# The head of a two-layer graph kernel: order of TensorE's uses, of the loads on two queues, and of ACT's steps

## What is computed

```
def _L0_gnn_ref(h, adj, simlar, W_proj, b_proj, W_gcn, b_gcn):
    sim = jnp.tanh(adj * simlar)                    # simlar is adj: tanh(adj^2)
    filt = sim * (adj > 0).astype(sim.dtype)
    ...                                             # the T = 350 largest of each row
    h2 = jnp.tanh(h @ W_proj + b_proj)
    feat = jax.nn.relu(new_adj @ (h2 @ W_gcn) + b_gcn)
    return feat

def _L1_gnn_ref(feats, node_adj, edge_adj, node_weight, node_bias, edge_weight, edge_bias):
    pos = jnp.matmul((node_adj > 0).astype(feats.dtype), feats)
    neg = jnp.matmul((node_adj < 0).astype(feats.dtype), feats)
    node_output = jnp.matmul(jnp.concatenate([pos, neg], axis=1), node_weight)
    node_output = node_output + node_bias * jnp.diagonal(edge_adj)[:, None]
    edge_output = jnp.matmul(jnp.matmul(edge_adj, feats), edge_weight)
    return node_output + edge_output + edge_bias * jnp.diagonal(node_adj)[:, None]

x = _layernorm(x + _L0_gnn_ref(x, adj, adj, ...), axis=-1)
x = _layernorm(x + _L1_gnn_ref(x, adj, adj, ...), axis=-1)
```

## Time and profile before

| | us |
|---|---|
| median of 3 runs | 619.83 |
| lowest and highest of them | 618.65, 620.12 |
| the profiled execution's own time | 618.95 |
| its span, first to last instruction | 617.2 |
| busy in the span: PE, DVE, ACT, POOL | 603.0, 472.7, 417.5, 186.9 |

### The profile page before, as it was taken

One profiled execution on the slowest core, in us unless ns is written; L12 is line 12 of the kernel. 1 busy time (PEld: TensorE's weight loads), 2 busy tenths in 40 slices (PEclk: granted clock), 3 DMA queues, 4 the chain that ended last, 5 costly groups with the idle time before them and its releaser, 6 DMA issues.

```text
span 617.2 us, 5685 instructions
## 1 busy us (share of the span) xinstructions
PE 603.0 (98%) x1970; PEld 344.5 (56%) x1970; DVE 472.7 (77%) x683; ACT 417.5 (68%) x297; POOL 186.9 (30%) x80
## 2 busy tenths in 40 slices
PE   7799999999999999999999999999999999999995
PEld 6644444444444444555555655655655656558994
DVE  2577879797887879986787697796787786887733
ACT  3387686868686786648884783883893884865850
POOL 0387796978879796200000000000000000000000
PEclk9799999999999999999999999999999999999998
DMA  8999999999999990047898399387486685783000
GB/s 236 336 343 343 336 281 314 273 327 276 323 292 309 291 236 1 1 137 193 234 248 241 107 252 254 100 244 220 135 252 174 172 243 147 210 242 110 2 17 19
DMA packets 141181, 130.65 MB, mean 212 GB/s; under 512 B 9443, under 2 KB 141158, under 8 KB 141158
## 3 DMA queue, kind: packets, MB, share of 16 engines
q1 hardware_dynamic: 74982, 66.22, 38.9%
q10 hardware_dynamic: 66176, 64.17, 37.4%
HBM read 128.27 MB, written 2.10 MB: 211 GB/s over the span
## 4 chain that ended last, share of the span: by engine, by line
PE 95%; DMA 2%; ACTq 1%; ACT 1%; DVE 0%; issue 0%; DVEq 0%
PE acc L939 36%; PE acc L953 33%; PE stage L962 10%; PE stage L961 10%; PE stage L953 2%; DMA x_rows<-in_x_dram 2%; PE to_rows L968 1%; PE to_rows L967 1%; ACTq L462 1%; PE stage L907 1%; PE to_rows L924 1%; ACT a_cols L525 0%; PE to_cols L913 0%; PE stage L902 0%; ACTq L465 0%
## 5 line engine op out<-in xcount | busy, mean ns | idle before, releaser
L592 DVE STREAM_TRANSPOSE a_cols<-a_rows 128x2048 f32<-128x2048 f32 x128 | 294.5, 2306 | 87.8 <-PE stage L962 53.0
L939 PE MATMUL acc<-a_cols,rhs 128*128 128x512 f32 x512 | 221.1, 592 | 0.7 <-ACT a_cols L525 0.7
L953 PE MATMUL acc<-a_cols,x_rows 128*128 128x512 f32 (+1 forms) x512 | 216.2, 565 | 0.0
L359 POOL TENSOR_TENSOR a_cols<-a_cols 128x1536 f32<-128x1536 f32 x64 | 175.3, 2749 | 63.7 <-DVE a_cols L592 62.7
L939 PEld LDWEIGHTS acc<-a_cols,rhs 128*128 128x128 f32 x512 | 96.7, 190 | 119.4 <-issue 119.4
L525 ACT ACTIVATE a_cols<-a_cols 128x2048 f32<-128x2048 f32 x64 | 122.4, 1912 | 53.4 <-POOL a_cols L359 52.3
L953 PEld LDWEIGHTS acc<-a_cols,x_rows 128*128 128x128 f32 x512 | 96.0, 189 | 86.3 <-issue 81.0
L541 ACT ACTIVATE a_rows<-a_rows 128x4096 f32<-128x4096 f32 x32 | 116.0, 3624 | 25.6 <-DVE a_cols L592 12.6
L961 PE MATMUL stage<-masks,x_hi 128*128 128x512 f32 (+1 forms) x288 | 126.8, 449 | 0.0
L544 ACT ACTIVATE a_rows<-a_rows 128x4096 f32<-128x4096 f32 x32 | 116.0, 3623 | 1.0
L962 PE MATMUL stage<-masks,x_lo 128*128 128x512 f32 (+1 forms) x288 | 103.1, 367 | 0.0
(11 more groups left out here) (103 smaller groups left out, 238.9 us busy)
## 6 DMA issues: line engine op xcount, KB each, us to landing
a_rows<-in_adj_dram SPq DMA_DIRECT2D x120, 512.0 KB, 9.0
a_rows<-in_adj_dram ACTq DMA_DIRECT2D x120, 512.0 KB, 10.1
out_dram<-n_rows SPq DMA_DIRECT2D x28, 64.0 KB, 8.5
x_rows<-in_x_dram SPq DMA_DIRECT2D x6, 128.0 KB, 4.1
x_rows<-in_x_dram ACTq DMA_DIRECT2D x6, 128.0 KB, 5.4
x_rows<-in_x_dram SPq DMA_DIRECT2D x4, 64.0 KB, 2.1
x_rows<-in_x_dram ACTq DMA_DIRECT2D x4, 64.0 KB, 2.4
diag<-in_adj_dram SPq DMA_DIRECT2D x16, 1.0 KB
```

Source lines behind the costliest of these rows:

```text
L359: nc.gpsimd.tensor_tensor(part, part, part, ALU.mult).then_inc(squared_pool, 1)
L592: nc.vector.transpose(half_out(hs), half_in(s, h % HALVES)).then_inc(turned[layer], 1)
L939: last = nc.tensor.matmul(acc[parity][:], rhs[:, b, :], a_cols[:, h % HSLOTS, k, :], start=(b == 0), stop=(b == BLOCKS - 1))
L953: last = nc.tensor.matmul(sums, x_rows[:, b, :], rows(a_cols[:, h % HSLOTS, k, :]), start=(b == 0), stop=(b == BLOCKS - 1))
```

## The change

- `USES`: the steps that groups 0 to 5 (x's parts 0 to 3) allow come ahead of the groups of x's last part. The new order is turn 0, turn 1, hid 0, turn 2, hid 1, turn 3, hid 2, rhs 0, turn 4, hid 3, rhs 1, turn 5, hid 4, rhs 2, hid 5, rhs 3, rhs 4, turn 6, rhs 5, turn 7, hid 6, hid 7, rhs 6, rhs 7.
- `by_dve`: ACT now also copies turn 7 and rhs 2.
- `EARLY`: the transposes of halves 0 to 2 of chunk 0 stand ahead of DVE's copies of rhs 4, 5 and 7.
- SP issues x's part 1 ahead of W_proj and its bias. ACT issues x's parts 1 and 2 ahead of W_gcn, and the bias of W_gcn behind x's last part, with a semaphore of its own; TensorE waits for the matrix alone, ACT for the bias ahead of chunk 0.
- ACT squares its part of half 0 behind the tanh of hid 6, inside the head.
- ACT's quarters of pieces 1 and 2 of chunk 0 go behind the tanhs of hid 4 to 7, those of piece 3 behind the tanhs of halves 0 and 1 of chunk 0, and those of chunk 1 behind the tanhs of halves 3, 5 and 7 (two pieces there). From chunk 1 on nothing changes.
- `hid` waits on TensorE through `emptied`, since a turn can now be copied by either engine.

```diff
@@ -66,7 +66,7 @@
     X_PARTS = [4, 4, 8, 8, 8]
     X_FIRST = 4
     WARM_UP = 7
-    EARLY = [("turn", 7), ("rhs", 4), ("rhs", 6)]
+    EARLY = [("rhs", 4), ("rhs", 5), ("rhs", 7)]
 
     ctx = ExitStack()
     with ctx:
@@ -218,6 +218,7 @@
         x_loaded = [sem(f"x_loaded{k}") for k in range(len(X_PARTS))]
         proj_loaded = sem("proj_loaded")
         gcn_loaded = sem("gcn_loaded")
+        b_gcn_loaded = sem("b_gcn_loaded")
         wl1_loaded = sem("wl1_loaded")
         a_loaded = [sem(f"a_loaded{k}") for k in range(SLOTS)]
         zeroed = sem("zeroed")
@@ -298,12 +299,17 @@
 
 
         GROUPS = BLOCKS // TILES
+        X_LAST = sum(X_PARTS[:X_FIRST]) // TILES
         turns, hids, rhss = ([(kind, g) for g in range(GROUPS)] for kind in ("turn", "hid", "rhs"))
         USES = turns[:2]
-        for k in range(GROUPS):
-            USES += hids[k:k + 1] + rhss[max(k - 2, 0):max(k - 1, 0)] + turns[k + 2:k + 3]
-        USES += rhss[GROUPS - 2:]
-        by_dve = [k == "turn" or (k == "rhs" and g not in (1, 3)) for k, g in USES]
+        for k in range(X_LAST):
+            USES += hids[k:k + 1] + rhss[max(k - 2, 0):max(k - 1, 0)] + turns[:X_LAST][k + 2:k + 3]
+
+        USES += rhss[X_LAST - 2:X_LAST - 1] + turns[X_LAST:X_LAST + 1] + rhss[X_LAST - 1:X_LAST] + turns[X_LAST + 1:]
+        for k in range(X_LAST, GROUPS):
+            USES += hids[k:k + 1] + rhss[k - 1:k] * (k > X_LAST)
+        USES += rhss[GROUPS - 1:]
+        by_dve = [(k == "turn" and g < GROUPS - 1) or (k == "rhs" and g not in (1, 2, 3)) for k, g in USES]
         HEAD = [stage[0][:], stage[1][:], stage[2][:], stage[3][:], to_cols[:],
                 to_rows[:].rearrange("p t f -> p (t f)")]
 
@@ -375,9 +381,10 @@
                         .then_inc(a_loaded[s], 16)
 
             load_x(0)
+            load_x(1)
             sp.dma_start(w_pg[:, 0, :], w_proj).then_inc(proj_loaded, 16)
             sp.dma_start(b_col[:, 0:1], b_proj.rearrange("(p a) -> p a", a=1)).then_inc(proj_loaded, 16)
-            for part in range(1, X_FIRST):
+            for part in range(2, X_FIRST):
                 load_x(part)
             load_piece((0, 0), 0)
             for part in range(X_FIRST, len(X_PARTS)):
@@ -471,15 +478,23 @@
             load_x(0)
             act.wait_ge(consts, 1)
             nc.scalar.activation(signs[:, 0:1], ones[:, 0:1], ACT.Tanh)
+            load_x(1)
+            load_x(2)
             act.dma_start(w_pg[:, 1, :], w_gcn).then_inc(gcn_loaded, 16)
-            act.dma_start(b_col[:, 1:2], b_gcn.rearrange("(p a) -> p a", a=1)).then_inc(gcn_loaded, 16)
-            for part in range(1, X_FIRST):
+            for part in range(3, X_FIRST):
                 load_x(part)
             load_piece((0, 0), 0)
             for part in range(X_FIRST, len(X_PARTS)):
                 load_x(part)
 
+            act.dma_start(b_col[:, 1:2], b_gcn.rearrange("(p a) -> p a", a=1)).then_inc(b_gcn_loaded, 16)
+
             act.wait_ge(proj_loaded, 32)
+            def square_rest(n):
+                rest = flat(a_cols, n % HSLOTS)[:, SQ_POOL:]
+                act.wait_ge(turned[0], n + 1)
+                nc.scalar.activation(rest, rest, ACT.Square).then_inc(squared_act, 1)
+
             for n, (kind, g) in enumerate(USES):
                 if by_dve[n]:
                     continue
@@ -487,13 +502,18 @@
                 if kind == "hid":
                     nc.scalar.activation(group(h_t, g), bank_of(n), ACT.Tanh, bias=b_col[:, 0:1])\
                         .then_inc(stage_act, 1)
-                    if g >= 2:
-                        load_quarter((0, 0), g // 2, ACT_QUARTERS[g % 2])
+
+                    if g >= 4:
+                        load_quarter((0, 0), g // 2 - 1, ACT_QUARTERS[g % 2])
+                    if g == 6:
+                        square_rest(0)
+                elif kind == "turn":
+                    nc.scalar.copy(group(feat_t, g), bank_of(n)).then_inc(stage_act, 1)
                 else:
                     nc.scalar.copy(rhs[:, g * TILES:(g + 1) * TILES, :],
                                    bank_of(n).rearrange("p (b f) -> p b f", f=F)).then_inc(stage_act, 1)
 
-            act.wait_ge(gcn_loaded, 32)
+            act.wait_ge(b_gcn_loaded, 16)
 
             def relu_out(chunk):
                 c, q, parity = chunk
@@ -514,16 +534,23 @@
                     n = c * HPC + h
                     hs = h % HSLOTS
                     act.wait_ge(turned[0], n + 1)
-                    if h % HALVES == HALVES - 1 and chunk is not LAST:
+                    if h % HALVES == HALVES - 1 and before and chunk is not LAST:
                         load_piece(rows_of(0, next_of(chunk)), h // HALVES)
-                    rest = flat(a_cols, hs)[:, SQ_POOL:]
-                    nc.scalar.activation(rest, rest, ACT.Square).then_inc(squared_act, 1)
+                    if h or before:
+                        square_rest(n)
                     if h == 7 and before:
                         high_part(before)
                     act.wait_ge(squared_act, n + 1)
                     act.wait_ge(squared_pool, n + 1)
                     nc.scalar.activation(a_cols[:, hs, :, :], a_cols[:, hs, :, :], ACT.Tanh)\
                         .then_inc(tanh_done, 1)
+                    if not before:
+                        if h < HALVES:
+                            load_quarter((0, 0), PIECES - 1, ACT_QUARTERS[h])
+                        elif h % HALVES == HALVES - 1:
+                            load_piece(rows_of(0, next_of(chunk)), h // HALVES - 1)
+                if not before:
+                    load_piece(rows_of(0, next_of(chunk)), PIECES - 1)
 
             each_chunk(layer0)
             relu_out(LAST)
@@ -903,11 +930,11 @@
                 elif kind == "hid":
                     if g == 0:
                         pe.wait_ge(proj_loaded, 32)
-                    pe.wait_ge(stage_dve, count_of("turn", g))
+                    emptied(pe, USES.index(("turn", g)))
                     last = nc.tensor.matmul(bank, w_pg[:, 0, :], group(feat_t, g), start=True, stop=True)
                 else:
                     if g == 0:
-                        pe.wait_ge(gcn_loaded, 32)
+                        pe.wait_ge(gcn_loaded, 16)
                     pe.wait_ge(stage_act, count_of("hid", g))
                     for k in range(TILES):
                         last = nc.tensor.matmul(bank[:, k * P:(k + 1) * P], blk(h_t, g * TILES + k),
```

## The result

| | before | after |
|---|---|---|
| median | 619.24 us (4 runs) | 627.45 us (4 runs, 623.81 to 631.59) |
| profiled execution, its span | 618.95, 617.2 us | 625.05, 623.3 us |
| ratio | | 1.0132 [1.0094, 1.0170] |

What follows compares the result with a forecast made beforehand. TensorE's unbroken stream bounds the kernel, so only its start counts: 11.48 us from x's landing becomes 6.7, 4.8 less, taking the profiled 618.95 to 614.2. Median forecast 615.0, own range 613.9 to 616.2; with rival 2, 613.7 to 617.6.

Steps and rivals of the forecast that it cites:

- S: Start of TensorE's unbroken stream at the first layer-0 product; forecast to move from 31.8 to 27.0 us.
- Order on TensorE: In the head, hid 5, rhs 3, rhs 4 fill the gap before turn 6: 2.64 us, plus 2.74 of slow clock.
- ACT's copy: In the head, ACT copies turn 7 in 0.59 us; hid 7 starts within 0.03 of TensorE being free: free.
- the square: ACT's square of half 0 inside the head: saves 0.66 us later, costs hid 7's tanh 0.35.
- DVE's transposes: Half 0's transpose ahead of rhs 4's copy: just hidden; piece 0 landing 1 us later would move the stream's start 0.8.
- rival 1: Clock falls anyway at the gap before turn 6: stream starts about 3.0 us later, 618.0; chance 0.11.
- x's last part at 20.2: In the head, the landing of x's last part was kept at 20.2 us, bounds 19.4 and 21.1.
- ACT's loads: Chunk 0's loads spread out, each still issued before its predecessor landed: landings taken as unchanged, 26.2, 32.5, 38.8 us.
- The cover: Time by which halves 2, 4, 6 are ready before TensorE wants them: 0.4, 1.0, 1.5 us; stall bound 0 to 2.
- The slower rival: Late loads hold ACT's queue back for good; 9 us late gives about 622.5; chance 0.04.
- rival 4: Chunk 0's pieces 2 and 3 land over 6.5 us later; beyond 6.3 to 6.5, each us costs one; chance 0.04.
- The rule I weighed: DMA engines alternate between queues with work, so a short ACT queue gives turns to SP; weighed against the spread loads.

Runs made afterwards that it cites:

- loads are placed anew: Changed kernel with ACT's loads re-placed: piece 1 behind hid 2, 3; piece 2 behind hid 4, rhs 3; chunk 1 behind halves 2, 4, 6, 7: 616.76 us.
- all loads back: Changed kernel with ACT's loads of chunks 0 and 1 returned to where they stood before the change: 619.14 us, ratio 1.0007.
- chunk 0's loads back: Changed kernel with ACT's chunk 0 loads where they were before, chunk 1's left late as in the change: 627.03 us, ratio 1.0116.
- late loads alone: Kernel before with only the change's late ACT loads, nothing else of the change: 632.73 us, ratio 1.0210.
- one half earlier: Changed kernel with ACT's chunk 0 loads back and chunk 1's behind the tanhs of halves 2, 4, 6 and 7: 616.23 us, ratio 0.9951.
- with the old order of x: Changed kernel with ACT's loads re-placed, and x, weights and W_gcn's bias issued in the order of the kernel before: 615.35 us, ratio 0.9944.

## Why the prediction was wrong

- **What bounds the kernel** (one stream of TensorE, all that counts is S, "as long as transfers keep up"): right, and the condition was the point.
- **Order on TensorE, ACT's copy, the square, DVE's transposes**: right. S is 6.6 us behind turn 6 in the changed kernel, 27.23 - 20.65 = 6.6 where loads are placed anew; 6.7 was summed. The clock stayed at 1.00 through a gap of 2.1 us before turn 6, so rival 1 didn't happen in the head of this profile. It did in a relative: with SP holding pieces 2 and 3 back the gap was 2.53 us, and the clock 0.50 from 24 to 26. In the changed kernel the lower clock came later, behind both waits of the stream, and cost 1.7 us each time.
- **x's last part at 20.2**: turn 6, which waits for it, starts at 21.33 in the changed kernel and at 20.3 to 24.2 in its relatives, against 20.32 and 20.25 in the two profiles of before. The bound of 21.1 was too tight. With the late loads in the old order of x it starts at 23.00. With the old loads in the new order it starts at 22.13 (all loads back) and at 20.34 (chunk 0's loads back), and these two kernels have the same head up to there: one program's executions differ by 1.8 us. So one profile of each doesn't show what moved x; left open.
- **ACT's loads: the step that failed.** I read "issued before its predecessor has landed" as enough and kept the landings of before. Two assumptions were in it. The first, that a queued transfer is ready to move when the one ahead of it ends; the quarter issued at 15.73 moved at 21.65, 5.9 us behind its issue, and the issue stood 3.9 us later than in the timeline of before (11.88). The second, that a pause of one queue costs little; SP's queue alone carried 202 GB/s where both carried 345. Summing the 4 us stretches from 8 to 64 us, the changed kernel moved 1.7 MB less than before, 5 us at 347 GB/s. The cover was 0.4, 1.0 and 1.5 us for halves 2, 4 and 6; pieces 1, 2 and 3 came 4.1, 3.9 and 4.6 us late. Undoing the loads takes the loss away (619.14), and the loads alone make one (632.73), so this step is shown to be the cause. That a late start makes up all of the lateness isn't shown: the thin tails of x's last part and of piece 3 have a part in it that no run separates.
- **The slower rival** named the right mechanism ("a queue standing empty for most of a piece's 6 us") and dismissed it with 0.04 because no issue time showed it. Its price was also wrong: it took pieces to be late once, against the 6.5 us of cover of the old stream start. But lateness is handed on, since a piece's place is reloaded only after its transpose: chunk 1's first piece was complete at 51.7 in the changed kernel, its second at 58.0. Before, the transpose of chunk 1's first half ran at 49.32 and waited for TensorE, not for a transfer. The changed kernel lost 6.1 us with pieces 3.9 to 4.6 us late, where rival 4 allowed 6.5 us for free; it also left out the slow clock behind each wait.
- **The rule I weighed.** I drew from the Trainium skill, "DMA: Bandwidth & Descriptors", Queues, rings and completion order (engines take turns between the queues that have work), that ACT's missing turns would go to SP's queue. The engines' time did go there: their share stayed at 113%, all of it for SP's packets. The bytes did not: SP's went from 0.33 to 0.38 MB in 1.9 us, not to 0.66. That same page of the Trainium skill, section Issuing engines are not separate DMA queues, says that issuing from several engines saves only the time of the issue; here two filled queues carried 345 GB/s and one 202, so the measurement decides against it.

A rival that I should have had is the opposite one: loads issued early stand for room on ACT (3.04 and 2.83 us) ahead of what TensorE waits for. Both sides leave a narrow place for each issue. By an estimate from these profiles it is at least 6 us before the queue runs out (the longest start was 6.0 us) and with no more than four quarters outstanding (an issue stood with five). Placed so, the kernel took 616.76 and 615.35 us, 0.3 and 0.6% under before.

## What to carry to other kernels

When a load is moved later, ask not whether it is issued before the transfer ahead of it has ended, but how long before, and compare it with the longest time from issue to first packet that any trace of the kernel shows; then price an empty queue as lost bandwidth, not as bandwidth lent to the other queue. Issues that share an engine with work have a cost on both sides: too early they stand for room ahead of that work, too late they starve the queue. Where a pipeline reloads a buffer only when it has been used, one late piece comes back in the next round, so a small edit of issue times can cost more than the stall that it first makes.

## What the runs showed of the hardware

- One full queue alone carried 202 GB/s (changed kernel, 19.7 to 21.6) and 207 (late loads alone, 27.0 to 31.8), with the DMA engines' share above 110%; two carried 345 to 350.
- Issue to first packet: at most 1.1 us with the other queue almost empty (one profile), 4 to 6 us with it holding two quarters or more (four profiles).
- An issue of 512 KB that found five quarters of its queue not yet landed (at 28.06 in the run with all loads back) held the engine for 3.04 us; one quarter takes 3.0 us at half of 347 GB/s. Later in the stream single issues took up to 3.9 us (chunk 0's loads back).
- One kernel can take two courses: 614.3 to 623.2 in the run one half earlier, 615.1 to 626.1 with the old order of x. The profiles, both of the longest execution, show stretches below 300 GB/s from 36 and 28 us on. The kernel before has such an execution too, 627.31 among 20 that else took 617.6 to 622.1, without a profile.
